# The recurrent layer of a two-layer decoder: head features stacked as high and low parts, scores in one rounded-f32 pass

## The chip, the core and the metric

The kernel runs on one core of a Trainium2 chip. TensorE (PE in the rows, PEld its weight loads) multiplies matrices, VectorE (DVE) and ScalarE (ACT) work elementwise, GpSimd (POOL) does so too and cannot touch the matmul results' memory (PSUM), SyncE (SP) issues DMAs. The metric is the time of one execution on the device in microseconds, the median of several.

## The reference

Two decoder layers over 4 batches of 256 tokens, width 256. Everything but the cross mixer of the second layer stays as it is. That mixer is a recurrent layer (an mLSTM) in its parallel form, with 16 heads of 16 features; the query is x, key and value are both the context:

```python
x3 = jnp.concatenate([q, k, v], axis=-1)
ig = (x3 @ Wi + bi).transpose(0, 2, 1)[..., None]
fg = (x3 @ Wf + bf).transpose(0, 2, 1)[..., None]
log_f = jax.nn.log_sigmoid(fg)             # cumulated over the tokens: fg_mat
log_D = log_fg + jnp.transpose(ig, (0, 1, 3, 2))      # causal, -inf above
max_log_D = jnp.max(log_D, axis=-1, keepdims=True)
D = jnp.exp(log_D - max_log_D)
qk = jnp.einsum('bhsd,bhtd->bhst', qh, kh) / jnp.sqrt(dh)
C = qk * D
normalizer = jnp.maximum(jnp.abs(C.sum(-1, keepdims=True)), jnp.exp(-max_log_D))
h = jnp.einsum('bhst,bhtd->bhsd', C / (normalizer + EPS), vh)
mu = h.mean(-1, keepdims=True)
hn = (h - mu) * jax.lax.rsqrt(((h - mu) ** 2).mean(-1, keepdims=True) + EPS) * ln_scale
```

## The kernel before

The program is a row of blocks; all engines meet at the end of each. Three blocks matter. In `layer1_lstm_load` SP issues two DMAs, and the block ends when they are issued. In `layer1_gates` PE forms both gates for all batches (L1241), ACT the log sigmoid, and VectorE the cumulated sums and maxima (L1276 to L1283), then the negated maximum in three bf16 parts (L1286 to L1293). SP copies these parts to rows of `nM_rows` with 12 DMAs (L1312), and the block ends when they have landed.

`layer1_lstm` is the recurrence: 4 batches of 16 heads, 64 heads in all, with keys on the partitions and queries along the row. The first and the last batch are written out, the two between are a loop. For each head:

- PE writes the exponent `l_z_ps` with two bf16 matmuls (L1386 the causal mask, L1387 the maximum), and ACT takes exp of it into `l_dec` in two instructions (L1471, L1472). Only 384 of 512 columns are needed, since the keys 128 to 255 are seen by the later queries alone.
- VectorE multiplies the transposed context by a column that is nonzero on the 16 rows of the head (`l_key`, L1502), and PE multiplies these 128 rows by xT in plain f32 (L1395 256 columns, L1397 128): the scores `l_qk_ps`.
- VectorE multiplies `l_dec` by `l_qk_ps` to `l_C` (L1554).

After four heads PE mixes the values with `l_C` (`mix`, L1414, 12 matmuls on 32 columns of the array), ACT keeps the result (L1453), PE turns it (L1423), ACT keeps that in `l_raw` (L1460). After a batch VectorE normalizes each head (13 instructions in `take`, `spread` and `scale`, L1508 to L1531), with one power on GpSimd (L1376, `l_rstd`) between them; they stand behind heads 4, 7 and 15 of the next batch. Each engine takes its instructions strictly in the order written. PE runs at most two heads ahead of VectorE, since the scores have two buffers; exponents and `l_dec` have four. Semaphores name what is waited for: `z_done`, `exped`, `qk_done`, `C_done`, `mixed`, `hT_kept`, `raw_kept`.

## Time and profile before

| | us |
|---|---|
| median of 3 runs (lowest, highest) | 1420.99 (1420.01, 1421.34) |
| span of the profiled execution | 1414.4 |
| what the median has beside the span | 6.6 |
| load block, first DMA issued | 914.3 |
| gates: first matmul, last DMA issued | 915.7, 944.0 |
| recurrence: first matmul, last result `h` | 945.7, 1052.5 |
| PE, VectorE, ACT, GpSimd busy in one batch of it (974 to 998) | 21.5, 19.9, 13.4, 5.5 of 24 |
| granted TensorE clock there | 1.00 of 2.4 GHz |

Only the three blocks differ between the kernels, so their stretch, 914 to 1053 us, is what is to be read. A time in a row is in us from the start of the span, durations follow it; in brackets stands how long the engine was idle before the instruction, and what ended that.

### The profile page before, as it was taken

To read this page: it belongs to the slowest core of one execution; us is meant where nothing else is said; L and a number is where in the kernel's file an instruction comes from. 1 tells how busy PE (TensorE), PEld (TensorE's weight loads), DVE (VectorE), ACT (ScalarE), POOL (GpSimd) and SP (SyncE) were. 2 spreads that over 40 slices of the span, in tenths; PEclk is the share of its full clock that TensorE was granted. 3 is DMA by queue.
4 is the path that set the end of the run, shared out by engine and by line. 5 is a ranking of instruction groups with operands and counts; after the bars stand their busy time and mean duration, and the time that the engine had idled before them with its cause. 6 is when DMAs were issued, how large, how long until landed. Compare 5 with 4: busy or idle time off the path is not lost. (4 is left out here: it accounts for less than half of the span.)

```text
span 1414.4 us, 20117 instructions
## 1 busy us (share of the span) xinstructions
PE 1156.9 (82%) x6280; PEld 883.5 (62%) x6280; DVE 723.0 (51%) x1850; ACT 480.2 (34%) x1324; POOL 411.8 (29%) x468
## 2 busy tenths in 40 slices
PE   5999999999660999086999999869946849999994
PEld 3777777778530887033777778737723537777773
DVE  5777787863440233220555561137864426566564
ACT  0333333341200232022555551125531234454442
POOL 3555555523535122640000000101141032342211
PEclk9999999999865899578999999979976879999997
DMA  9300000000012897214000000000001041112000
GB/s 334 146 23 22 22 22 22 11 1 1 1 37 89 267 299 252 83 43 144 10 14 12 12 1 1 19 5 2 0 1 36 1 134 45 45 52 83 0 1 30
DMA packets 72976, 82.16 MB, mean 58 GB/s; under 512 B 8417, under 2 KB 63527, under 8 KB 72912
## 3 DMA queue, kind: packets, MB, share of 16 engines
q1 hardware_dynamic: 59200, 50.94, 11.9%
q0 software_dynamic: 5632, 15.73, 3.2%
q10 hardware_dynamic: 8080, 14.69, 2.8%
q8 instruction: 34, 0.56, 0.2%
q14 instruction: 30, 0.25, 0.1%
HBM read 60.22 MB, written 22.02 MB: 58 GB/s over the span
## 5 line engine op out<-in xcount | busy, mean ns | idle before, releaser
L346 PE MATMUL a_proj_ps<-xT,a_w 128*128 128x512 f32 x256 | 121.8, 610 | 9.7 <-DMA a_w<-in_L_attn_Wv_dram 9.5
L248 ACT ACTIVATE a_probs<-a_score_ps,a_nmax 128x128 f32<-128x128 f32 x128 | 47.1, 368 | 207.3 <-DVE a_nmax L241 207.3
L221 PEld LDWEIGHTS a_turn_ps<-ident,a_probs 128*128 128x128 f32 x384 | 47.9, 142 | 65.7 <-DVE a_probs L259 32.8
L438 POOL TENSOR_TENSOR a_qk<-a_by_cos,a_by_sin 128x512 f32<-128x512 f32 x64 | 85.2, 1330 | 5.0
L104 POOL TENSOR_SCALAR ln_d_var<-ln_d_ssq 128x1 f32<-128x1 f32 x8 | 1.5, 192 | 283.6 <-ACT ln_d_sq L98 283.4
L221 PE MATMUL a_turn_ps<-ident,a_probs 128*128 128x128 f32 x384 | 65.0, 279 | 22.0 <-DVE a_probs L259 22.0
L346 PEld LDWEIGHTS a_proj_ps<-xT,a_w 128*128 128x128 f32 x256 | 47.3, 195 | 55.3 <-issue 49.8
L265 ACT ACTIVATE a_probsT<-a_turn_ps 128x384 f32<-128x384 f32 x128 | 62.5, 488 | 54.4 <-PE a_turn_ps L221 54.4
L240 DVE TENSOR_REDUCE a_nmax<-a_score_ps 128x1 f32<-128x128 f32 x128 | 36.6, 286 | 76.3 <-PE a_score_ps L214 75.7
L340 PEld LDWEIGHTS a_proj_ps<-a_w,xT 128*128 128x128 f32 x512 | 63.7, 196 | 15.5 <-issue 7.4
L434 POOL TENSOR_TENSOR a_by_sin<-a_swapped,sin_q 128x512 f32<-128x512 f32 x32 | 40.7, 1271 | 112.1 <-DVE a_swapped L394 112.1
L899 DVE TENSOR_TENSOR e_actT<-e_silu,e_up_ps 128x256 f32<-128x256 f32 x32 | 13.5, 421 | 113.0 <-ACT e_silu L883 113.0
L340 PE MATMUL a_proj_ps<-a_w,xT 128*128 128x128 f32 x512 | 64.2, 280 | 6.1 <-DVE a_swapped L394 6.1
L258 DVE TENSOR_SCALAR a_probs<-a_probs,a_rtotal 128x128 f32<-128x128 f32 x128 | 65.6, 512 | 4.5
L1092 PE MATMUL a_proj_ps<-xT,a_w 128*128 128x512 f32 x128 | 61.5, 605 | 3.2 <-DMA a_w<-in_L_attn_w_q_dram 3.2
L843 PE MATMUL e_up_ps<-e_rowsT,e_w 128*128 128x256 f32 x256 | 63.5, 393 | 0.0
L2111 DVE TENSOR_TENSOR m_xe<-m_xe_ps,xT 128x512 f32<-128x512 f32 x32 | 21.9, 691 | 79.4 <-PE m_xe_ps L1854 64.1
L833 PE MATMUL e_turn_ps<-ident,e_rows 128*128 128x128 f32 x128 | 21.2, 292 | 47.4 <-DMA e_rows<-slots 47.4
L259 DVE TENSOR_SCALAR a_probs<-a_probs,a_rtotal 128x256 f32<-128x256 f32 x128 | 59.6, 466 | 0.0
L250 ACT ACTIVATE a_probs<-a_score_ps,a_nmax 128x256 f32<-128x256 f32 x128 | 59.6, 466 | 0.0
L1177 PE MATMUL p_y_ps<-wo,attnT 128*128 128x256 f32 x256 | 55.5, 379 | 0.8 <-PEq L1071 0.8
L527 PE MATMUL t_y_ps<-wo,attnT 128*128 128x256 f32 x256 | 55.9, 379 | 0.0
(373 smaller groups left out, 3140.9 us busy)
## 6 DMA issues: line engine op xcount, KB each, us to landing
slots<-zeros ACTq DMA_DIRECT2D x4, 2048.0 KB, 16.6
e_rows<-slots SPq DMA_DIRECT2D x32, 256.0 KB, 4.2
e_w<-in_L_ffn_w_dram SPq DMA_DIRECT2D x32, 256.0 KB, 3.8
out_slots<-e_out POOLq DMA_DIRECT2D x32, 256.0 KB, 4.8
e_w<-in_L_ffn_w_dram SPq DMA_DIRECT2D x32, 128.0 KB, 3.8
m_up_w<-in_up_dram SPq DMA_DIRECT2D x8, 512.0 KB, 3.9
a_w<-in_L_attn_Wq_dram SPq DMA_DIRECT2D x16, 128.0 KB, 2.2
a_w<-in_L_attn_Wk_dram SPq DMA_DIRECT2D x16, 128.0 KB, 2.3
```

Source lines behind the costliest of these rows:

```text
L221: last = pe.transpose(self.turn_ps[:, r, j * P:(j + 1) * P], self.probs[:, r, j * P:(j + 1) * P], self.k.ident[:, :])
L250: act.activation(self.probs[:, r, P:P + S], self.score_ps[:, r, P:P + S], ACT.Exp, bias=self.nmax[:, r, 1:2], accum_out=self.total[:, r, 1 ...
L258: dve.tensor_scalar(self.probs[:, r, 0:P], self.probs[:, r, 0:P], self.rtotal[:, r, 0:1], None, ALU.mult)
L259: dve.tensor_scalar(self.probs[:, r, P:P + S], self.probs[:, r, P:P + S], self.rtotal[:, r, 1:2], None, ALU.mult).then_inc(self.normed, 1)
L265: act.activation(self.probsT[:, b % 2, :], self.turn_ps[:, b % 2, 0:CAUSAL], ACT.Copy).then_inc(self.turned_kept, 1)
L340: last = pe.matmul(proj_ps[:, c % 2, t * HD:(t + 1) * HD], k.xT[:, kc, half * HALF + t * P:half * HALF + (t + 1) * P], w[:, par, 2, kc, :] ...
L346: last = pe.matmul(proj_ps[:, c % 2, :], w[:, par, 0 if what == "q" else 1, kc, :], k.xT[:, kc, half * HALF:(half + 1) * HALF], start=kc = ...
L438: pool.tensor_tensor(qk[:, par, 0 if what == "q" else 1, half * HALF:(half + 1) * HALF], by_cos[:, r, :], by_sin[:, r, :], ALU.add).then_i ...
L527: last = pe.matmul(y_ps[:, t % 2, 0:D], k.ctxT[:, h, t * P:(t + 1) * P], k.wo[:, h, :], start=h == 0, stop=h == H - 1)
L843: last = pe.matmul(up_ps[:, r % 2, j * CAP:(j + 1) * CAP], w13[:, r, c, j * I0:(j + 1) * I0], rowsT[:, r % 2, c * CAP:(c + 1) * CAP], star ...
L1092: last = pe.matmul(proj_ps[:, half, :], w[:, par, c, :], k.xT[:, c, half * HALF:(half + 1) * HALF], start=c == 0, stop=c == DC - 1)
L1177: last = pe.matmul(y_ps[:, t % 2, 0:D], k.ctxT[:, h, t * P:(t + 1) * P], k.wo[:, h, :], start=h == 0, stop=h == H - 1)
```

## The change

- **Stacks.** The scores no longer use a masked key. `key_stack` holds the 16 key features of a head four times on 64 rows: twice their high part (rounded f32, F32R) and twice the rest (low part). `x_stack` holds the query features as high, low, high, low. One pass over 64 rows then sums all four products. Two heads lie on one tile of 128 rows, so the matmul of an odd head uses the lower half of the array (`tile_position`).
- **Building `x_stack`.** In the gates block ACT rounds a spreading matrix and x, VectorE takes the low part of x, PE spreads both with 32 F32R matmuls of 512 columns, ACT copies five results and VectorE three.
- **Building `key_stack`.** The context comes in stacked order from DRAM, 1 MB a batch, into two buffers (`raw`, in the place of the attention's output weights `wo`). ACT rounds a batch (`stack_high`, 128x8x256), then GpSimd subtracts on rows 32 to 63 and on rows 96 to 127 (`stack_low`, twice 32x8x256). Batch 0 is built in the gates block, batch 1 at the start of the recurrence, batches 2 and 3 when ACT has reached head 8 of the batch before.
- **Recurrence.** `l_key` and its instruction are gone. All 64 heads are written out. The scores have three buffers, the exponents three, `l_dec` six. The mask matmul writes 256 columns in place of 384. `mix` comes behind the scores of head n+2 when n % 4 is 1; ACT keeps its results behind exp of a head with n % 4 = 0.
- **Group norm.** The same 13 instructions are spread over heads 9 to 14 of the next batch, and the last two come behind head 6 of the batch after that; for the third batch they come after the last head.
- **Loads.** SP issues three more DMAs in the load block (the spreading matrix and two raw batches), and two in the recurrence.

```diff
+def stack_load(sp, k, I, b):
+
+    sp.dma_start(k.raw[:, b % 2], I["ctx_stack"][:, b * S:(b + 1) * S].rearrange("(c p) s -> p c s", p=P)
+                 ).then_inc(k.raw_in[b % 2], 16)
+
+
+def stack_high(act, k, b):
+
+    act.wait_ge(k.raw_in[b % 2], 16 * (b // 2 + 1))
+    act.activation(k.key_stack[:, :, b * S:(b + 1) * S], k.raw[:, b % 2], ACT.Copy).then_inc(k.stack_high, 1)
+
+
+def stack_low(pool, k, b):
+
+    pool.wait_ge(k.stack_high, b + 1)
+    for i, rows in enumerate((slice(P // 4, P // 2), slice(3 * P // 4, P))):
+        at_least(pool, k.stack_low, 2 * b + i)
+        pool.tensor_tensor(k.key_stack[rows, :, b * S:(b + 1) * S], k.raw[rows, b % 2],
+                           k.key_stack[rows, :, b * S:(b + 1) * S], ALU.subtract).then_inc(k.stack_low, 1)
...
+                pe.wait_ge(spread_ready, 1)
+                pe.wait_ge(x_low, DC)
+                for c in range(STACKS):
+                    at_least(pe, kept_a, min(c - 1, BY_ACT))
+                    at_least(pe, kept_v, c - 1 - BY_ACT)
+                    for half in range(2):
+                        tokens = slice(half * HALF, (half + 1) * HALF)
+                        for part, x in enumerate((x_p.h, x_p.l)):
+                            last = pe.matmul(st_ps[:, c % 2, half, :], k.spread[:, part, c % 4, :],
+                                             x[:, c // 4, tokens], start=part == 0, stop=part == 1)
+                    last.then_inc(stacked, 1)
...
+                act.wait_ge(k.spread_in, 16)
+                act.activation(k.spread[:, :, :, :], k.spread_w[:, :, :, :], ACT.Copy).then_inc(spread_ready, 1)
+                act.wait_ge(k.xT_ready, k.xT_count)
+                for c in range(DC):
+                    act.activation(x_p.h[:, c, :], k.xT[:, c, :], ACT.Copy).then_inc(x_high, 1)
...
+                stack_high(act, k, 0)
+                for c in range(BY_ACT):
+                    act.wait_ge(stacked, c + 1)
+                    act.activation(k.x_stack[:, c, :], st_ps[:, c % 2].rearrange("p a s -> p (a s)"), ACT.Copy
+                                   ).then_inc(kept_a, 1)
...
+                for c in range(DC):
+                    dve.wait_ge(x_high, c + 1)
+                    dve.tensor_tensor(x_p.l[:, c, :], k.xT[:, c, :], x_p.h[:, c, :], ALU.subtract).then_inc(x_low, 1)
...
+                for c in range(BY_ACT, STACKS):
+                    dve.wait_ge(stacked, c + 1)
+                    dve.tensor_copy(k.x_stack[:, c, :], st_ps[:, c % 2].rearrange("p a s -> p (a s)")
+                                    ).then_inc(kept_v, 1)
...
             def _(pool):
                 pool.memset(k.nM_rows[:, :, :], 0.0).then_inc(v_zero, 1)
+                pool.wait_ge(v_zero, 1)
+                stack_low(pool, k, 0)
...
-    RING = 4
+    RING = 3
+    DECS = 6
     GROUP = P // VW
     GROUPS_B = LH // GROUP
     NQ = QT * LH
+    STRIP = 4 * LW
...
+        STEPS = 11
+        AT_HEAD = {9: (0, 1, 2, 3), 10: (4,), 11: (5, 6), 12: (7,), 13: (8,), 14: (9,)}
...
+            @block.sync
+            def _(sp):
+                for b in range(2, B):
+                    sp.wait_ge(k.stack_low, 2 * (b - 1))
+                    stack_load(sp, k, I, b)
+
             @block.gpsimd
             def _(pool):
                 pool.memset(v_b[:, :, :, :], 0.0).then_inc(v_clear, 1)
                 pool.wait_ge(v_clear, 1)
                 pool.memset(v_b[:, :, :, LW:LW + 1], 1.0).then_inc(v_ones, 1)
+                pool.wait_ge(v_ones, 1)
+                stack_low(pool, k, 1)
                 for b in range(B):
+                    if b + 2 < B:
+                        at_least(pool, rstd_done, b)
+                        stack_low(pool, k, b + 2)
                     pool.wait_ge(var_done, b + 1)
+                    at_least(pool, k.stack_low, 2 * (b + 3) if b + 2 < B else 0)
...
+                def exponents(n):
+
+                    if n >= LH * B:
+                        return
+                    b, h = n // LH, n % LH
+                    at_least(pe, exped, n - RING + 1)
+                    z = z_ps[:, n % RING, :]
+                    pe.matmul(z.rearrange("p (a s) -> p a s", a=2)[:, :, 0:P], k.ident_bf[:, :],
+                              k.after_bf[:, :].rearrange("p (a s) -> p a s", a=2), start=True, stop=False,
+                              skip_group_check=True)
+                    pe.matmul(z[:, 0:CAUSAL], k.sel[:, h, :], k.nM_rows[:, b, :], start=False, stop=True,
+                              skip_group_check=True).then_inc(z_done, 1)
+
+                def products(n):
+
+                    if n >= LH * B:
+                        return
+                    at_least(pe, C_done, n - RING + 1)
+                    b, h = divmod(n, LH)
+                    if h == 0:
+                        pe.wait_ge(k.stack_low, 2 * (b + 1))
+                    c, strip = h // 2, h % 2 * STRIP
+                    rows = slice(strip, strip + STRIP)
+                    for keys_at, x_at, to in ((b * S, slice(b * S, (b + 1) * S), slice(0, S)),
+                                              (b * S + P, slice(b * S + P, (b + 1) * S), slice(S, CAUSAL))):
+                        last = pe.matmul(qk_ps[:, n % RING, to], k.key_stack[rows, c, keys_at:keys_at + P],
+                                         k.x_stack[rows, c, x_at], start=True, stop=True, tile_position=(strip, 0))
+                    last.then_inc(qk_done, 1)
...
+                for n in range(RING - 1):
+                    exponents(n)
+                products(0)
+                products(1)
+                for n in range(LH * B):
+                    exponents(n + RING - 1)
+                    products(n + 2)
+                    G = n // GROUP - 1
+                    if n % GROUP == 1:
+                        if G >= 1:
+                            turn(G - 1)
+                        if G >= 0:
+                            mix(G)
+                turn(B * GROUPS_B - 2)
+                mix(B * GROUPS_B - 1)
+                turn(B * GROUPS_B - 1)
...
+                stack_high(act, k, 1)
+                for n in range(LH * B):
+                    b, h = n // LH, n % LH
+                    if n % LH == 0:
+                        act.wait_ge(batch_ready, b + 1)
+                    if h == LH // 2 and 0 < b < B - 1:
+                        stack_high(act, k, b + 1)
+                    act.wait_ge(z_done, n + 1)
+                    at_least(act, C_done, n - DECS + 1)
+                    act.activation(dec[:, n % DECS, 0:S], z_ps[:, n % RING, 0:S], ACT.Exp,
+                                   bias=g_b[:, b % 2, 0, h:h + 1])
+                    act.activation(dec[:, n % DECS, S:CAUSAL], z_ps[:, n % RING, S:CAUSAL], ACT.Exp,
+                                   bias=g_b[:, b % 2, 1, h:h + 1]).then_inc(exped, 1)
+                    G = n // GROUP - 2
+                    if n % GROUP == 0 and G >= 0:
+                        if G >= 1:
+                            keep_raw(G - 1)
+                        keep_hT(G)
...
+                    at_least(dve, exped, LH * (b - 1))
+                    dve.tensor_copy(g_b[:, b % 2], k.g_tok[:, :, ROWS * b:ROWS * b + LH]).then_inc(batch_ready, 1)
...
+                for n in range(LH * B):
+                    b, i = divmod(n, LH)
+                    h = i
+                    dve.wait_ge(exped, n + 1)
+                    dve.wait_ge(qk_done, n + 1)
+                    if n % GROUP == 0:
+                        at_least(dve, mixed, n // GROUP - 1)
+                    dve.tensor_tensor(C[:, h % (2 * GROUP), :], dec[:, n % DECS, :], qk_ps[:, n % RING, 0:CAUSAL],
+                                      ALU.mult).then_inc(C_done, 1)
+                    if b > 0:
+                        if i == 2:
+                            dve.wait_ge(mixed, GROUPS_B * b)
+                            values(b)
+                        for j in AT_HEAD.get(i, ()):
+                            group_norm(b - 1, j)
+                    if b > 1 and i == 6:
+                        for j in (10, 11):
+                            group_norm(b - 2, j)
+                    if i == 8 and b + 1 < B:
                         fetch(b + 1)
+                for j in (10, 11):
+                    group_norm(B - 2, j)
+                for j in range(12):
+                    group_norm(B - 1, j)
...
+            sp.dma_start(k.spread_w[:, :, :, :], I["spread"]).then_inc(k.spread_in, 16)
+            stack_load(sp, k, I, 0)
+            stack_load(sp, k, I, 1)
```

On TensorE, the heads around a mix in the first batch of before (`l_z_ps` exponents, `l_qk_ps` scores, `l_hT_ps` mix, `l_turn_ps` turn):

```order
L1386 MATMUL l_z_ps<-after_bf,ident_bf 128x384
L1387 MATMUL l_z_ps<-nM_rows,sel 128x384
L1414 MATMUL l_hT_ps<-l_C,l_v_b 32x128 x12
L1395 MATMUL l_qk_ps<-xT,l_key 128x256
L1397 MATMUL l_qk_ps<-xT,l_key 128x128
L1386 MATMUL l_z_ps<-after_bf,ident_bf 128x384
L1387 MATMUL l_z_ps<-nM_rows,sel 128x384
L1395 MATMUL l_qk_ps<-xT,l_key 128x256
L1397 MATMUL l_qk_ps<-xT,l_key 128x128
L1423 MATMUL l_turn_ps<-ident,l_hT 128x128 x2
```

and now:

```order
L1453 MATMUL l_z_ps<-after_bf,ident_bf 128x2x128
L1456 MATMUL l_z_ps<-nM_rows,sel 128x384
L1471 MATMUL l_qk_ps<-x_stack,key_stack 128x256
L1471 MATMUL l_qk_ps<-x_stack,key_stack 128x128
L1493 MATMUL l_turn_ps<-ident,l_hT 128x128 x2
L1485 MATMUL l_hT_ps<-l_C,l_v_b 32x128 x12
```

The mix has moved behind the scores, and the turn of the group before stands in front of it.

On GpSimd, everything in the gates block and the recurrence of before:

```order
L1304 MEMSET nM_rows 128x1536
L1371 MEMSET l_v_b 128x1024
L1373 MEMSET l_v_b 128x32
L1376 TENSOR_TENSOR l_rstd<-l_var,minus_half 128x32 x4
```

and now, where `key_stack<-wo,key_stack` is the subtraction of the low part (two a batch):

```order
L1360 MEMSET nM_rows 128x1536
L1225 TENSOR_TENSOR key_stack<-wo,key_stack 32x8x256 x2
L1428 MEMSET l_v_b 128x1024
L1430 MEMSET l_v_b 128x32
L1225 TENSOR_TENSOR key_stack<-wo,key_stack 32x8x256 x4
L1439 TENSOR_TENSOR l_rstd<-l_var,minus_half 128x32
L1225 TENSOR_TENSOR key_stack<-wo,key_stack 32x8x256 x2
L1439 TENSOR_TENSOR l_rstd<-l_var,minus_half 128x32 x3
```

The power of a batch now stands behind the subtractions for the batch after the next.

On VectorE, behind head 7 of the second batch, now:

```order
L1623 TENSOR_TENSOR l_C<-l_dec,l_qk_ps 128x384
L1563 COPY l_g_b<-g_tok 128x32
L1623 TENSOR_TENSOR l_C<-l_dec,l_qk_ps 128x384
L1576 SCALAR_TENSOR_TENSOR l_rnorm<-l_raw 128x32
L1579 TENSOR_TENSOR l_norm<-l_rnorm,least 128x32
L1581 TENSOR_SCALAR l_normed<-l_norm 128x32
L1583 RECIPROCAL l_rnorm<-l_normed 128x32
L1623 TENSOR_TENSOR l_C<-l_dec,l_qk_ps 128x384
L1585 TENSOR_TENSOR l_hv<-l_raw,l_rnorm 128x512
L1589 TENSOR_REDUCE l_hsum<-l_hv 128x32
L1623 TENSOR_TENSOR l_C<-l_dec,l_qk_ps 128x384
```

The copy of the gates for the next batch stands behind head 8, the group norm starts behind head 9, and no `l_key` stands between.

## Rows read from the trace of the kernel before

**Rows 1.** Windows: one batch; then a pause of TensorE, and ten microseconds later.

```profile
974.00:998.00 24.00, 21.48 (x207) 17.15 (x206) 19.91 (x51) 13.41 (x43) 5.47 (x1) 1.00 0.01 2
1090.00:1095.00 5.00, 1.10 (x3) 0.19 (x1) 4.76 (x8) 0.60 (x1) 0.00 (x0) 1.00 0.01 2
1100.00:1105.00 5.00, 4.31 (x22) 4.27 (x21) 0.00 (x0) 2.48 (x3) 0.00 (x0) 0.50 0.01 3
```

**Rows 2.** Timeline (start, duration, engine, line) around one mix of the recurrence.

```profile
988.38 0.33 PE L1386 MATMUL l_z_ps<-after_bf,ident_bf 128*128 128x384 bf16 x1
988.54 0.33 PE L1387 MATMUL l_z_ps<-nM_rows,sel 128*128 x1
...
988.79 0.86 PE L1414 MATMUL l_hT_ps<-l_C,l_v_b 128*32 128x128 f32 x24
...
989.59 0.70 PE L1395 MATMUL l_qk_ps<-xT,l_key 128*128 x2
...
990.00 0.47 ACT L1471 ACTIVATE l_dec<-l_z_ps,l_g_b 128x256 f32<-128x256 f32 x1
...
990.76 0.55 DVE L1554 TENSOR_TENSOR l_C<-l_dec,l_qk_ps 128x384 f32<-128x384 f32 x1 [1.30 <-ACT l_dec L1472]
...
991.24 0.35 DVE L1502 TENSOR_SCALAR l_key<-cT,head_of 128x256 f32 x1
```

**Rows 3.** Timeline of TensorE: two rounded-f32 matmuls of 256 columns.

```profile
1195.17 0.28 PE L1852 MATMUL m_down_ps<-m_down_l,m_act_h 128*128 128x256 f32 x1
1195.30 0.28 PE L1853 MATMUL m_down_ps<-m_down_h,m_act_h 128*128 128x256 f32 x1
```

**Rows 4.** Timeline: start of the recurrence, heads 0 and 16, the last two heads.

```profile
945.66 0.48 PE L1386 MATMUL l_z_ps<-after_bf,ident_bf 128*128 128x384 bf16 x1 [7.41 <-PEq L1232]
...
950.15 0.55 DVE L1554 TENSOR_TENSOR l_C<-l_dec,l_qk_ps 128x384 f32<-128x384 f32 x1 [1.02 <-PE l_qk_ps L1397]
...
971.43 0.56 DVE L1554 TENSOR_TENSOR l_C<-l_dec,l_qk_ps 128x384 f32<-128x384 f32 x1 [1.18 <-PE l_qk_ps L1397]
...
1036.93 1.18 DVE L1554 TENSOR_TENSOR l_C<-l_dec,l_qk_ps 128x384 f32<-128x384 f32 x2 [1.56 <-ACT l_dec L1472]
```

**Rows 5.** Timeline of the last group norm: first, power, last.

```profile
1040.49 0.21 DVE L1508 SCALAR_TENSOR_TENSOR l_rnorm<-l_raw 128x32 f32<-128x32 f32 x1 [1.06 <-ACT l_raw L1460]
...
1045.66 5.42 POOL L1376 TENSOR_TENSOR l_rstd<-l_var,minus_half 128x32 f32<-128x32 f32 x1 [10.33 <-DVE l_var L1526]
...
1051.83 0.69 DVE L1531 TENSOR_TENSOR h<-l_hs,head_scale 128x512 f32<-128x512 f32 x1
```

**Rows 6.** Instructions by tile (ns min/median/max): rounding on ACT, subtraction on GpSimd.

```profile
L2062 ACT ACTIVATE m_up_h<-m_up_w x8: 1039/1046/1046, 1143.0 to 1353.2; 128x1024 fp32r<-128x1024 f32 x8
L1970 POOL TENSOR_TENSOR m_up_l<-m_up_w,m_up_h x8: 2379/2409/2409, 1144.1 to 1354.3; 128x1024 fp32r<-128x1024 f32 x8
```

**Rows 7.** Timeline: VectorE while GpSimd works; then two of its lines by tile.

```profile
72.40 1.27 POOL L434 TENSOR_TENSOR a_by_sin<-a_swapped,sin_k 128x512 f32<-128x512 f32 x1
72.45 1.37 DVE L259 TENSOR_SCALAR a_probs<-a_probs,a_rtotal 128x256 f32<-128x256 f32 x1
...
L259 DVE TENSOR_SCALAR a_probs<-a_probs,a_rtotal x128: 340/348/1376, 35.3 to 849.8; 128x256 f32<-128x256 f32 x128
...
L2145 DVE TENSOR_TENSOR m_act<-m_silu,m_up x16: 676/677/1424, 1165.0 to 1388.7; 48x512 f32<-48x512 f32 x16
```

**Rows 8.** Timeline of the gates block, from the logarithm to the DMAs.

```profile
927.85 0.42 ACT L1260 ACTIVATE g_ln<-g_e 128x256 f32<-128x256 f32 x1
...
932.88 0.69 DVE L1283 TENSOR_TENSOR_SCAN g_M<-ones,g_g 128x256 f32<-128x256 f32 x1
...
933.60 0.29 DVE L1286 TENSOR_SCALAR g_nM<-g_M 128x256 f32<-128x256 f32 x1
...
936.42 7.58 SPq L1312 DMA_DIRECT2D nM_rows<-g_parts  x12
```

**Rows 9.** Timeline: the second DMA issue of the load block.

```profile
914.68 0.42 SPq L2243 DMA_DIRECT2D after_bf<-in_after_bf_dram  x1
```

234 lines of the change are left out of this document (83 added, 151 removed).

## The prediction

> **What bounds the kernel now.** I read the page first (its table stands above), then windows over the recurrence, then timelines in order of time. In a batch of 24 us TensorE is busy 21.5 and VectorE 19.9 at full clock [rows 1], so neither alone is the bound: they hand over to each other. Around a mix the reader sees how. The mix starts 0.25 us behind the exponents, holds TensorE 0.8 us (988.79 to 989.59), and VectorE sits idle 1.30 us until exp arrives [rows 2]. Batch 0 runs 21.3 us without a group norm (heads 0 to 16), all 64 heads take 88.0 us (950.15 to 1038.11), and the first head starts 4.5 us into the block [rows 4]. Behind the last head come 2.4 us until the last group norm starts, then 12.0 us to `h` [rows 5]. In the gates block the end is set by VectorE's chain: the maximum at 932.88, its negation from 933.60, 2.8 us to the last part, then 12 DMAs in 7.6 us, landed at 945.6 [rows 4, 8].
>
> **The change part by part.** The terms are differences to the profiled execution; the 6.6 us that the median has beside the span are taken as they are.
>
> *Loads, +1.4.* Three more issues stand before the end of the load block, at 0.42 us and a short gap each [rows 9]: 3 x 0.47.
>
> *Recurrence without disturbance, -26.6.* A rounded-f32 pass of 256 columns starts 0.13 us after the one before [rows 3]; I take 0.13 + 0.06 for the scores of a head (by column count for the narrow one; if it ran as four passes it would be 0.2, which adds 0.15 a group of four heads). The exponents take 0.16 for 384 columns [rows 2], so 0.11 + 0.16. VectorE needs for a head between 0.48 (next start behind an `l_C`) [rows 2] and 0.59 (half of 1.18) [rows 4], I take 0.5. Then a group of four heads runs in a loop that I close over the mix: end of `l_C` of head n-1, scores 0.2, turn 0.25 (two f32 transposes of 128 columns, an estimate from [rows 3]), mix with its start gap 0.25 + 0.8 [rows 2], exponents of head n+3 0.27 and 0.2 to their end, exp 0.76 (990.00 to 990.76) [rows 2], `l_C` 0.55: 3.3 us. The copies that ACT keeps of the results lie beside it. Batch 0 is four such groups and slower by 0.3 while the clock is low: 13.5. In later batches the group norm fills the gaps: its first ten steps take 5.2 us (1040.49 to 1045.66) [rows 5], the last two 1.4, the two copies 0.6. Heads 8 to 11 then cost VectorE 4 x 0.5 + 3.6 = 5.6, heads 12 to 15 2.0 + 1.7 = 3.7, heads 0 to 3 stay at 3.3, heads 4 to 7 take 3.3 (3.4 with the two late steps): 15.9, 16.0, 16.0. Sum 61.4 against 88.0.
>
> *Start of the recurrence, -1.6.* ACT first rounds batch 1: 1.046 us for 1024 elements [rows 6], so 2.0 for 2048. Exp is at 2.8, head 0 at 2.9 instead of 4.5 [rows 4].
>
> *Tail, +4.0.* The third batch's variance is now ready behind head 14 of the last batch. The power takes 5.4 us [rows 5], so its last two steps start 5.0 us behind the last `l_C` and end at 6.4, where the last group norm started at 2.4 before. All that follows is unchanged.
>
> *GpSimd against VectorE.* One subtraction of 128x1024 takes GpSimd 2.41 us [rows 6]; the new ones have 2048 elements on 32 partitions, I take 4.7 each (a little under twice), 9.4 a batch. What they do to VectorE decides. At 72.45 a `tensor_scalar` of VectorE that takes 0.35 alone takes 1.37, just until a subtraction-like instruction of GpSimd (72.40, 1.27 long) is over, and this line's maximum is 1.376 [rows 7]. A `tensor_tensor` with both inputs in SBUF shows the same (0.68 alone, 1.42 at most) [rows 7]. `l_C` reads PSUM, reductions and reciprocals have one input, and they should go on; nearly every other instruction of the group norm and of the gates chain is of the two kinds that wait. The Trainium skill says it outright (SBUF — State Buffer, section Who interferes with whom): VectorE instructions with two SBUF inputs, or in a two-port mode, exclude a GpSimd instruction that reads SBUF for its whole length, whichever comes first. The trace agrees at 1.27 us; that it holds at four times that length no row shows.
>
> - Gates, +6.7. ACT is through with the logarithm at 929.7 (1.4 late), rounds batch 0 until 931.6, GpSimd subtracts to 936.3. The maximum (two SBUF inputs) would start at 934.3, so it runs from 936.3 to 937.0; GpSimd's second subtraction has been queued since 936.4 and gets in first, as in the pair at 72.40. The negation starts at 941.7, the last part is ready 2.8 later at 944.5, where it would have been at 937.8 [rows 8]. Bounds: 0 if nothing excludes, 2.1 if the chain keeps its turn. The 32 matmuls, the eight copies of x and batch 0's subtractions end before the DMAs land.
> - Batch 0, +0.6: the copy of the gates behind head 8 meets the rest of batch 1's subtractions.
> - Batches 1 and 2, +7.8 and +8.1. ACT rounds the next batch when it reaches head 8, GpSimd starts at about `l_C` of head 8. Of its 9.4 us only heads 8 and 9 (some 1.6 us) run beside; the gate copy and the first group norm step wait for the rest, and all of the group norm comes afterwards.
> - Low clock after these pauses, +3.5. TensorE idles some 4 us twice. After a pause of about that size it is granted 0.50 at 86% busy [rows 1]: 1.2 of 2.4 GHz. At that level a group with a mix takes it 5.8 us (scores and exponents 3.6, turn and mix 2.2) against 3.3 to 5.6 that VectorE needs. I take 1.75 a pause; bounds 0 and 4.
>
> Sum: 1.4 - 26.6 - 1.6 + 4.0 + 6.7 + 16.5 + 3.5 = +3.9, so 1425.
>
> Another rule speaks against the change: the Trainium skill (TensorE: Matmul & The Clock Gate, section A second HAM failure mode: psum-queue depth-cycling) tells of a kernel in which brief idling between groups of matmuls made the clock swing. Here TensorE would be idle a quarter of the time even without the exclusions; the trace has no such stretch in the recurrence (clock 1.00) [rows 1]. It is the last rival.
>
> **The rivals.**
> *The exclusion costs half* (faster). GpSimd gets in only between VectorE's instructions or is shorter on 32 partitions, so the chain in the gates keeps its turn (2.1) and batches 1 and 2 lose 4 to 5 each, without a fall of the clock: 1.4 - 26.6 - 1.6 + 4.0 + 2.1 + 10 = -10.7, 1410. For it: the late instruction of VectorE gets its turn at once when GpSimd's ends. Against it: at 72.45 VectorE was 0.05 us late and waited the full length [rows 7], and the second subtraction is queued while VectorE still runs.
> *No exclusion* (clearly faster): the two streams pass each other, only the readiness of the low parts costs 2 us, since the subtractions end about when head 14 asks for the next batch: -26.6 - 1.6 + 1.4 + 4.0 + 2 = -20.8, 1400. Against it stand both lines of [rows 7].
> *The clock stays low* through the undisturbed groups too: 2.5 us (5.8 against 3.3) for each of ten groups without group norm, less the 3.8 that the sum has for it: +21 on the forecast, 1446; half of it 1435. For it: idle time of TensorE in every group; against it: the full clock at 21.5 of 24 us [rows 1], and that TensorE at 1.2 GHz would have no idle time left in these groups.
> Beside these, `values` of batch 0 may lose its turn to batch 1's first subtraction (VectorE leads by less than 0.1 us): +4, within the range. The change does what it says if the scores' matmuls are single passes; even as four passes it is only 1 to 2 us.
>
> **How the numbers follow.** Forecast 0.62 (own range 1416 to 1433), half exclusion 0.18 (1404 to 1416), none 0.10 (1395 to 1404), low clock 0.10 (1433 to 1448). The range 1407 to 1437 leaves out the third, a part of the second and half of the last. A measurement can tell 0.2%, 2.8 us, from no change: faster than 1418.2 are the second and third and a tenth of the first, 0.33; within, 0.17; slower, 0.50.
>
> **What would show it.** Right: subtractions of GpSimd near 4.7 us; the first group norm instruction behind head 9 with a duration of several us, ending with a subtraction; the negation in the gates block late by 6 to 7; in batch 3, where GpSimd subtracts nothing, 16 us; a granted clock below 1.00 in the second half of batches 1 and 2; the last group norm 6 to 7 us behind the last `l_C`. Wrong: group norm instructions of normal length beside subtractions (then 1400), GpSimd instructions that are themselves stretched, batches over 18 us without a subtraction.

## The result, and the profile after

The changed kernel takes 1439.5 us (median of 4 runs, 1434.4 to 1450.8) against 1420.5 (1416.1 to 1421.3) for the kernel before: a ratio of 1.016, 95% interval 1.012 to 1.021. Slower was right, but 19 us and not 4: the time lies 2.5 us outside the range of 1407 to 1437. It also varies from run to run by 16 us, where the kernel before varies by 5 in its four runs (by 10 and 12 in the 19 and 22 runs beside the first eight experiments).

The profiled execution of the changed kernel is the fastest of its four. The two profiled executions differ by 18.2 us in their spans (1432.6 and 1414.4), and `h` is complete 18.2 us later, so all of it arises up to the end of the recurrence:

| term | predicted | between the profiles |
|---|---|---|
| stages ahead of the changed blocks | 0 | +1.5 |
| loads | +1.4 | +1.6 |
| gates | +6.7 | +6.0 |
| start of the recurrence, to its first product | -1.6 | -1.8 |
| first to last product | -6.6 (88.0 to 81.4) | +6.6 (88.0 to 94.6) |
| tail, to `h` | +4.0 | +4.3 |

Every term that was forecast, but for the products, came out within 0.7 us. The 1.5 us ahead of the changed blocks are a difference that I can't assign.

The gates block, in the timeline of VectorE and GpSimd (start, duration, engine, line), answers to [rows 8]:

```profile
936.02 2.45 DVE L1335 TENSOR_TENSOR_SCAN g_M<-ones,g_g 128x256 f32<-128x256 f32 x1
938.51 4.51 DVE L1338 TENSOR_SCALAR g_nM<-g_M 128x256 f32<-128x256 f32 x1
...
933.36 9.50 POOL L1225 TENSOR_TENSOR key_stack<-wo,key_stack 32x2048 fp32r<-32x2048 f32 x2 [13.41 <-ACT key_stack L1217]
```

The scan takes 2.45 us instead of 0.69 and ends with GpSimd's first subtraction; the second gets in ahead of the negation, which takes 4.51 instead of 0.29 and ends with it at 942.9. In batch 1 (VectorE's timeline; the subtractions run from 983.86 to 992.95) the reader sees the same twice, then an instruction of normal length once GpSimd is through:

```profile
984.91 3.51 DVE L1563 COPY l_g_b<-g_tok 128x32 f32<-128x32 f32 x1
988.33 0.54 DVE L1623 TENSOR_TENSOR l_C<-l_dec,l_qk_ps 128x384 f32<-128x384 f32 x1
988.80 4.22 DVE L1576 SCALAR_TENSOR_TENSOR l_rnorm<-l_raw 128x32 f32<-128x32 f32 x1
993.05 0.19 DVE L1579 TENSOR_TENSOR l_norm<-l_rnorm,least 128x32 f32<-128x32 f32 x1
```

TensorE over the same time, in the windows view (columns: window, its length, then busy time and count of instructions for TensorE's matmuls, its weight loads, VectorE, ACT and GpSimd, granted clock, DMA share, GB/s), answers to [rows 1]:

```profile
954.00:966.00 12.00, 11.25 (x58) 5.85 (x58) 4.86 (x10) 7.43 (x17) 9.85 (x4) 0.50 0.26 87
967.00:982.00 15.00, 15.00 (x151) 8.86 (x154) 8.73 (x17) 11.76 (x39) 0.00 (x0) 1.00 0.22 72
988.00:990.00 2.00, 0.82 (x4) 0.41 (x4) 2.00 (x3) 0.00 (x0) 1.92 (x2) 1.00 0.00 0
992.00:998.00 6.00, 3.25 (x11) 1.77 (x11) 5.83 (x13) 2.44 (x8) 0.95 (x1) 0.50 0.00 1
998.00:1022.00 24.00, 24.00 (x155) 12.82 (x154) 14.16 (x20) 12.31 (x32) 12.99 (x3) 0.50 0.00 1
1022.00:1037.00 15.00, 13.08 (x75) 7.19 (x78) 10.02 (x20) 6.77 (x20) 6.91 (x2) 0.50 0.00 1
1038.00:1050.00 12.00, 11.46 (x102) 6.56 (x100) 10.13 (x23) 9.43 (x30) 0.00 (x0) 1.00 0.00 1
```

The clock is at 0.50 (1.2 GHz) in the first 12 us of the recurrence, falls again in the pause of batch 1 (in windows of 2 us it is 1.00 from 988, 0.55 from 990 and 0.50 from 992), and then stays there for 47 us, 24 of them with TensorE busy in all of the 24. The products of batches 0 to 3 take 18.0, 26.1, 30.5 and 19.9 us. A group with its mix takes 7.1 us there. And at full clock a group takes 4.2, not 3.3. TensorE's timeline shows why:

```profile
974.20 0.28 PE L1453 MATMUL l_z_ps<-after_bf,ident_bf 128*128 128x256 bf16 x1
974.32 0.33 PE L1456 MATMUL l_z_ps<-nM_rows,sel 128*128 128x384 bf16 x1
974.57 0.44 PE L1471 MATMUL l_qk_ps<-x_stack,key_stack 64*128 64x256 f32 x2
974.95 0.28 PE L1453 MATMUL l_z_ps<-after_bf,ident_bf 128*128 128x256 bf16 x1
```

From start to start a head takes 0.75 us: 0.12, then 0.25 (0.16 by its 384 columns) until the scores start, then 0.38 (0.16 by columns) until the next exponents. I had 0.47. Four times 0.75, 0.37 for the turn and 0.80 for the mix are the 4.2: TensorE has become the bound.

### The profile page after: what moved, and what is told of

The parts are those of the page before. It is cut to its first block and busy times, and to the rows that moved or that the text cites. A ratio compares the mean times of both kernels' runs of the same rounds, so it can differ in the third digit from the quotient of the medians.

```text
span 1432.6 us, 19649 instructions
## 1 busy us (share of the span) xinstructions
PE 1166.2 (81%) x6184; PEld 870.3 (61%) x6184; DVE 730.1 (51%) x1791; ACT 494.9 (35%) x1336; POOL 448.0 (31%) x476
## 5 line engine op out<-in xcount | busy, mean ns | idle before, releaser
L340 PEld LDWEIGHTS a_proj_ps<-a_w,xT 128*128 128x128 f32 x512 | 63.7, 196 | 15.5 <-issue 7.4
## 6 DMA issues: line engine op xcount, KB each, us to landing
slots<-zeros ACTq DMA_DIRECT2D x4, 2048.0 KB, 17.1
```

Of the source, the lines that this page charges most:

```text
L340: last = pe.matmul(proj_ps[:, c % 2, t * HD:(t + 1) * HD], k.xT[:, kc, half * HALF + t * P:half * HALF + (t + 1) * P], w[:, par, 2, kc, :] ...
```

## The experiments

In the texts on record a "theory" is what I held at that moment. Times are medians, with the lowest and highest run behind them; the kernel before was measured beside them each time (medians 1416.7 to 1417.6), and ratios are to these. What I read off each trace first is the time from the first to the last product (88.0 before, 94.6 after) and the stretches at 0.50.

**1. Small subtractions** (`x1_small_low`). The low parts are left out but for 8 columns:

```diff
-        pool.tensor_tensor(k.key_stack[rows, :, b * S:(b + 1) * S], k.raw[rows, b % 2],
-                           k.key_stack[rows, :, b * S:(b + 1) * S], ALU.subtract)
+        pool.tensor_tensor(k.key_stack[rows, 0, b * S:b * S + 8], k.raw[rows, b % 2, 0, 0:8],
+                           k.key_stack[rows, 0, b * S:b * S + 8], ALU.subtract)
```

> The changed kernel, but GpSimd's subtractions of the low part run over 8 columns of one chunk instead of 2048 elements (most low parts are left out; everything else is as it was). Theory: GpSimd's long instructions hold up VectorE (6.0 us in the gates block, 7.3 and 6.5 in batches 1 and 2), the two pauses of TensorE that follow take its clock to 0.50, and with the pauses gone it stays at 1.00 from about 966 on: a group of four heads takes 4.2 us instead of 7.1, batches 1 to 3 about 17 us each instead of 25, 30.5 and 19.9. Sum -6 -24 = 1409, clock 1.00 from the tenth microsecond of the recurrence to its end. Rival 1 (the clock falls by the new instruction mix itself, 64-row scores and no key masks, whatever pauses): the gates lose their 6 us, but the clock goes down again somewhere in batch 1 and batches take 25 to 28 us: 1433 or more. Rival 2 (the chip lowers the clock while GpSimd runs its long instructions, and they make no one wait): as the theory in time, but then the warmed kernel of this call would not help.

Measured: 1415.2 (1408.5 to 1423.2), ratio to before 0.999 (0.997 to 1.002); 87.6 us for the products. So by the medians the subtractions cost 24 us in all, give or take 8 by the two intervals; the profiled executions differ by 15.4, 7.0 of it in the products. But the clock did not do what the theory said:

```profile
948.00:1002.00 54.00, 53.85 (x311) 28.65 (x311) 22.67 (x48) 29.60 (x77) 5.19 (x7) 0.50 0.13 40
1003.00:1037.00 34.00, 32.25 (x323) 18.70 (x326) 26.50 (x58) 26.77 (x80) 7.21 (x4) 1.00 0.01 1
```

Without any pause it is at 0.50 from the start for 54 us, at 53.85 us of busy TensorE, and then at 1.00. No pause is needed for it to stay low. This speaks for the cause that rival 1 names, though not for its 1433. The second window also gives batches at full clock without exclusion: 18.5 and 17.1 us between the products of heads 32, 48 and the last.

**2. Idle matmuls in the pauses** (`x3_warm`), in batches 1 and 2 ahead of the scores:

```diff
+    def filler(n, count):
+        if count:
+            pe.wait_ge(exped, n + 1)
+        for _ in range(count):
+            pe.matmul(z_ps[:, n % RING, 0:S], k.ident_bf[:, :], k.after_bf[:, :], start=True, stop=True)
+    FILL = {9: 16, 10: 40}
...
+    if n // LH in (1, 2):
+        filler(n, FILL.get(n % LH, 0))
```

> The changed kernel with idle matmuls for TensorE in its two pauses: behind head 9 sixteen and behind head 10 forty bf16 matmuls of 256 columns, in batches 1 and 2 alone, into a bank that the next exponents overwrite. The exclusion stays as it is (7.3 and 6.5 us). Theory (the pause of TensorE, and nothing else, takes the clock down, and in the mix of this recurrence it doesn't come back before 1037): the clock stays at 1.00, batch 1 as long as now or 1 us longer, batch 2 about 24.5 instead of 30.5, batch 3 17 instead of 19.9, so 1430. Rival (GpSimd's load, or the mix of work, sets the clock): the clock falls in spite of the matmuls, which then take up to 24 us themselves at 0.43 us less each: 1440 to 1450.

Measured: 1439.1 (1432.8 to 1445.1), as the changed kernel. The trace shows two opposite things, which cancel in the time. This execution was at 0.50 for 40 us from 952, where the changed kernel's was for 12 at its start, and its batches 0 and 1 took 23.9 and 30.2 us instead of 18.0 and 26.1. But with the pauses filled the clock stayed at 1.00 through both of them, and batches 2 and 3 took 25.2 and 17.1 us instead of 30.5 and 19.9, as the theory has them. So a pause does take the clock down in this mix. The idle matmuls did not bring it back: it rose at 993, over 2 us ahead of the first of them (995.5). In between it fell once more, for 3 us from 1007, with TensorE busy for 2.58 of the 3 us before.

```profile
952.00:992.00 40.00, 38.52 (x216) 20.62 (x220) 14.16 (x28) 22.07 (x57) 10.37 (x4) 0.50 0.16 54
993.00:1006.00 13.00, 12.89 (x112) 9.13 (x110) 11.65 (x14) 5.96 (x19) 8.80 (x2) 0.99 0.00 1
```

**3. Scores over all rows** (`x4_full_rows`). Each score adds up two heads:

```diff
-    last = pe.matmul(qk_ps[:, n % RING, to], k.key_stack[rows, c, keys_at:keys_at + P],
-                     k.x_stack[rows, c, x_at], start=True, stop=True, tile_position=(strip, 0))
+    last = pe.matmul(qk_ps[:, n % RING, to], k.key_stack[:, c, keys_at:keys_at + P],
+                     k.x_stack[:, c, x_at], start=True, stop=True)
```

> The changed kernel, but each score matmul takes all 128 rows of the stacks instead of the 64 of one head (it adds up the scores of two heads; the same columns, the same number of instructions, no place on the array given). In the trace of the changed kernel a head takes TensorE 0.75 us at full clock: 0.12 and 0.25 for the exponents, 0.38 for the scores, where my sum had 0.47. Theory (the place on the array costs: the weights for 64 rows can't be loaded while a 128-row matmul still runs, 0.1 us in front of the first and 0.1 in front of the second): a head takes 0.55 to 0.60, a group 3.5 instead of 4.2, and with more rows in use the clock comes back sooner after a pause; 1439 - 16 groups x 0.6 = 1429 or less. Rival (a rounded-f32 pass has this cost anyway, by its weight load of 0.19 us or by a second pass): 0.75 a head stays, and so does 1439.

Measured: 1419.1 (1416.4 to 1423.0), the theory and more, 20 us less than the changed kernel with the same subtractions and pauses; 79.9 us for the products. In TensorE's timeline a head now takes 0.48, and the scores start at once:

```profile
971.90 0.28 PE L1453 MATMUL l_z_ps<-after_bf,ident_bf 128*128 128x256 bf16 x1
972.02 0.33 PE L1456 MATMUL l_z_ps<-nM_rows,sel 128*128 128x384 bf16 x1
972.05 0.48 PE L1471 MATMUL l_qk_ps<-x_stack,key_stack 128*128 128x256 f32 x2
972.38 0.28 PE L1453 MATMUL l_z_ps<-after_bf,ident_bf 128*128 128x256 bf16 x1
```

(A weight load ahead of its turn is counted with its matmuls, so their start is too early by a little; the distance from exponents to exponents is what counts.) Behind each pause the clock is at 0.50 too, but it is back 6 to 8 us after TensorE starts again (956.3 to 962.2, 990.2 to 996.3, 1015.7 to 1023.8). In windows:

```profile
956.00:962.00 6.00, 5.74 (x25) 4.79 (x26) 3.01 (x7) 5.38 (x12) 4.42 (x3) 0.50 0.52 175
962.00:980.00 18.00, 16.46 (x213) 12.78 (x210) 13.02 (x22) 15.87 (x46) 6.00 (x2) 0.99 0.19 60
...
988.00:996.00 8.00, 4.72 (x36) 3.05 (x36) 7.83 (x17) 2.63 (x8) 1.35 (x1) 0.50 0.00 1
996.00:1006.00 10.00, 8.92 (x106) 6.44 (x98) 6.53 (x13) 8.99 (x25) 6.21 (x2) 0.98 0.01 2
```

**4. The kernel before, with the subtractions' time added** (`x8_before_excl`), behind head 9 of batches 1 and 2:

```diff
+    pool.wait_ge(exped, LH * (b + 1) + 9)
+    for i in range(2):
+        pool.tensor_tensor(idle_b[0:32, :], idle_a[0:32, :], idle_b[0:32, :], ALU.subtract)
```

> The kernel before, with two more GpSimd subtractions over 2048 elements on 32 rows from when ACT has passed head 9, in batches 1 and 2, on tiles of their own that nobody needs: the same 9.1 us of GpSimd as in the changed kernel. Theory: VectorE's instructions of two SBUF inputs wait for them (about 4 us each time one meets one: +4 to +8 a batch), TensorE pauses, and its clock falls to 0.50; at 90% busy in this older mix of full-row matmuls it comes back after about 8 us, as at the start of the recurrence (945 to 953), so +3 for each: 1420.5 + 12 + 6 = 1438. Rival 1 (any pause of this size costs the clock until near the end, whatever the mix): +25 to +35. Rival 2 (nothing of the exclusion carries over because the group norm stands elsewhere there): 1420 to 1425.

Measured: 1435.8 (1434.4 to 1438.6), ratio 1.0145 (1.012 to 1.017): the theory. The products take 104.2 us. The exclusion is at work here too, in the timelines of VectorE and GpSimd:

```profile
995.49 2.75 DVE L1513 TENSOR_SCALAR l_key<-cT,head_of 128x256 f32 x1
998.16 0.54 DVE L1565 TENSOR_TENSOR l_C<-l_dec,l_qk_ps 128x384 f32<-128x384 f32 x1
998.62 4.59 DVE L1541 TENSOR_TENSOR l_hs<-l_hc,l_rstd 128x512 f32<-128x512 f32 x1
...
993.43 9.23 POOL L1387 TENSOR_TENSOR l_idle_b<-l_idle_a,l_idle_b 32x2048 f32<-32x2048 f32 x2
```

With its full-row scores the clock is back soon: in windows of 2 us, TensorE starts again in that from 1006, at 0.50, and has 0.55 in that from 1010 and 1.00 behind it; the second time it is 5 us. Behind its pause in batch 1 the changed kernel stayed at 0.50 for 47 us.

**5. Gates and tail** (`x26_gates_tail`).

```diff
                 pool.wait_ge(v_zero, 1)
+                pool.wait_ge(nm_done, 1)
                 stack_low(pool, k, 0)
...
-                for j in (10, 11):
-                    group_norm(B - 2, j)
-                for j in range(12):
-                    group_norm(B - 1, j)
+                for j in range(10):
+                    group_norm(B - 1, j)
+                for b in (B - 2, B - 1):
+                    for j in (10, 11):
+                        group_norm(b, j)
```

> The changed kernel with two edits far apart, read apart in the trace. In the gates block GpSimd's first two subtractions wait until VectorE has made the negated maximum and the last `nm`; in the tail the last two steps of the third batch stand between the last batch's variance and its scaling, in the 5.4 us in which VectorE waits for the power. Theory: the maximum's scan takes 0.7 instead of 2.45 and the negation 0.3 instead of 4.51, the last part is ready 6.0 earlier and the recurrence starts 6 earlier; the last group norm starts 2.4 behind the last product instead of 6.6, so 4.2 less in the tail. Rival for the gates: the subtractions only move behind, and hold up the copies and the turned gates until the block ends as late as before: 0 to 2 gained. Rival for the tail: the power of the third batch itself is late for the last batch's, 0 gained. Sum by the theory -10; where the clock of TensorE comes back differs from run to run by up to 40 us (in the trace of the changed kernel it was at 0.50 for 59 us, in the other runs more), so 1422 to 1436.

Measured: 1437.2 (1428.7 to 1443.9). By the time alone this is inconclusive. In the trace scan and negation are short again:

```profile
934.27 0.69 DVE L1335 TENSOR_TENSOR_SCAN g_M<-ones,g_g 128x256 f32<-128x256 f32 x1
934.99 0.29 DVE L1338 TENSOR_SCALAR g_nM<-g_M 128x256 f32<-128x256 f32 x1
```

The last part is ready 6.0 us earlier, as the theory has it: from the start of the scan to the first DMA 3.6 us (934.27 to 937.82) instead of 9.5 (936.02 to 945.55). Of these the recurrence gets 4.9: from the scan to its first matmul 13.8 us instead of 18.7. GpSimd's two subtractions, moved behind, end at 947.8, just ahead of that matmul (948.1), so the rival holds for 1.1 us. The first product comes at 950.8 instead of 957.5, but 1.8 us of this lie ahead of the scan.

But the profiled execution was at 0.50 from 952 to the end of the recurrence: 110.2 us for the products, the worst case of the changed mix. Since mix and turn are slow then, the last group norm starts 5.4 us behind the last product; the tail is to be read in experiment 8.

**6. No exclusion at all** (`x7_best`). VectorE makes the low part over 128 rows at once, and the work stands where engines are free:

```diff
-    act.activation(k.key_stack[...], k.raw[:, b % 2], ACT.Copy)
+    act.activation(k.key_stack[...], k.raw[:, b % 2], ACT.Identity, scale=k.flip[:, 0:1])   # -1 high, +1 low rows
...
+    dve.scalar_tensor_tensor(k.key_stack[:, at, ...], k.raw[:, b % 2, at], k.is_low[:, 0:1],
+                             k.key_stack[:, at, ...], ALU.mult, ALU.subtract)                  # four pieces
+    HIGH_AT = {8: 2, 18: 3}
+    LOW_AT = {1: 1, 2: 1, 3: 1, 4: 1, 9: 2, 10: 2, 11: 2, 12: 2, 20: 3, 21: 3, 22: 3, 23: 3}
```

> A version of the changed kernel without the exclusion: the low part is made by VectorE with one instruction over all 128 rows in four pieces of 0.7 us a batch (ACT rounds with the sign turned on the high rows, and VectorE takes raw x 0 or 1 less that), batch 0 in the shadow of the DMAs in the gates block, the others between heads of batches 0 and 1; batch 1 is rounded in the gates block; the tail as in the kernel beside it. Theory: as the kernel with small subtractions (1415.2) less the tail's 4.2 and the 2 us of the rounding: 1409, and as there the clock of TensorE is at 0.50 from the start of the recurrence for 10 to 55 us, since a mix of 64-row scores doesn't bring it back. Rival: VectorE's pieces, 8 us in all, are not hidden and eat the gain: 1415 or more.

Measured: 1410.8 (1398.4 to 1413.0), ratio 0.994 (0.992 to 0.996), faster than before; 0.50 for the 38 us from 952, then 1.00; products 81.2 us. As the theory.

**7. The same, warmed** (`x12_best_warm`): `for _ in range(60)` an idle matmul at the end of TensorE's part of the gates block.

> The same version with sixty idle bf16 matmuls of 256 columns for TensorE at the end of the gates block, while the DMAs of the negated maximum are on their way (6.4 us at full clock, 13 at half). Theory (the mix of the recurrence can keep the clock but hardly wins it back): the recurrence starts at 1.00 and stays there, since no pause comes, a group takes 4.2 us all through: 67 to 69 us from the first to the last product against 94.6 in the changed kernel, so 1401. Rival (the mix itself can't keep the clock): it falls in the first 20 us of the recurrence all the same, and the time is that of the kernel beside it, 1409, or 5 more if the matmuls run at half clock and are not done when the block ends.

Measured: 1412.8 (eleven runs from 1405.1 to 1418.1, one of 1430.6), no better. The theory falls, the rival holds. The recurrence does start at 1.00, and the clock falls all the same, twice, without a pause: TensorE was busy for 4.57 of the 6 us before the first fall (at 958) and for 3.30 of the 4 us before the second.

```profile
948.00:956.00 8.00, 6.96 (x58) 5.15 (x55) 0.76 (x3) 2.41 (x8) 1.10 (x2) 1.00 0.22 70
...
958.00:972.00 14.00, 14.00 (x85) 7.62 (x86) 9.33 (x18) 8.84 (x21) 0.00 (x0) 0.52 0.23 75
972.00:988.00 16.00, 15.81 (x164) 9.04 (x163) 11.47 (x26) 13.10 (x37) 0.00 (x0) 1.00 0.01 3
988.00:992.00 4.00, 3.30 (x28) 1.90 (x31) 3.93 (x9) 3.25 (x10) 0.00 (x0) 1.00 0.01 2
992.00:1008.00 16.00, 16.00 (x111) 8.48 (x100) 7.58 (x16) 6.91 (x21) 5.43 (x1) 0.50 0.00 1
```

**8. No exclusion, and full rows** (`x9_best_full`). x is kept twice, the other head's 64 rows at zero, so that a 128-row matmul yields one head:

```diff
+    pool.memset(k.x_stack[rows, at].bitcast(F32), 0.0)
-    k.key_stack[rows, c, keys_at:keys_at + P], k.x_stack[rows, c, x_at], ..., tile_position=(strip, 0)
+    k.key_stack[:, c, keys_at:keys_at + P], k.x_stack[:, h % 2, c, x_at], ...
```

> The version without the exclusion, and scores over all 128 rows: x is kept twice, with the other head's 64 rows at zero (GpSimd clears them, ACT and VectorE make 16 copies of 1.0 us instead of 8). Theory: a head takes TensorE 0.47 instead of 0.75 (0.46 to 0.47 in the kernel with full rows), a group some 3.3 to 3.5 instead of 4.2, limited by VectorE and by the loop over the mix, and the clock is back within 6 to 8 us of the start, as in the kernel with full rows: 62 to 65 us from the first to the last product, 1395 to 1398. Rival 1: the doubled copies of x don't fit beside the DMAs of the gates block and push the start by up to 8 us: 1403 to 1406. Rival 2: with TensorE faster VectorE (0.5 a head, 5.2 for a group norm, 2.8 for a batch's low part) is the bound and nothing more than 3 us is won over the version with 64 rows at full clock: 1399.

Measured: 1399.7 (1399.0 to 1400.3), ratio 0.987 (0.985 to 0.990): 18 us faster than the kernel before and 40 than the changed one, and without its scatter. The products take 63.8 us, and TensorE starts at 954, and the clock is up from 958.5:

```profile
952.00:957.00 5.00, 3.05 (x14) 2.51 (x14) 2.19 (x6) 1.83 (x6) 1.11 (x2) 0.50 0.39 124
957.00:1020.00 63.00, 52.55 (x633) 37.50 (x632) 54.84 (x119) 52.28 (x154) 10.87 (x2) 0.99 0.08 25
```

TensorE is idle a sixth of the 63 us and keeps its clock. The last group norm starts 2.4 us behind the last product (1020.5 to 1022.9), as before, and the third batch's last steps lie in the wait for the power: the tail's 4.2 us are gone. The products are faster by more than the 3 us of rival 2: 63.8 against the 69.4 that 64-row scores need at full clock (worked out below). Rival 1 holds for 6 us, which are still to be had here: the copies of x end at 952.6, and from the maximum's scan to the first product it takes 21.6 us (935.1 to 956.7) instead of the 15.5 of experiment 6 (938.0 to 953.5).

**9. The same, warmed** (`x13_full_warm`), with the sixty matmuls.

> The version with full rows (1399.7) and the sixty idle matmuls at the end of the gates block. Its recurrence ran at 0.50 for its first 4 to 5 us only, and TensorE has idle time in every window of it. Theory: those few microseconds become 1.00 and 1 to 2 us are won, 1398, if the matmuls are over when the DMAs have landed. Rival: they are not over (they stand behind the turned gates, and the copies of x run until 953 here), and push the start: 1402 to 1405.

Measured: 1406.7 (1402.7 to 1407.5), 7 us slower: the rival. The clock is at 1.00 from 946 on, but the products take the same 63.8 us, and the first of them comes at 960.1, 3.4 us late. In this mix the few cold microseconds cost nothing that shows. The profiled execution is 3.2 us longer in span than that of experiment 8, which is this delay; what adds the rest in the median is open.

**10. One idle matmul a head** (`x16_best_fill`), added to the version of experiment 6:

```diff
     exponents(n + RING - 1)
+    if n < LH * B - 2:
+        pe.wait_ge(exped, n + 1)
+        pe.matmul(z_ps[:, n % RING, 0:S], k.ident_bf[:, :], k.after_bf[:, :], start=True, stop=True)
     products(n + 2)
```

> The version without the exclusion and with 64-row scores (1410.8, clock 0.50 from 954 to 990) with one idle 128-row bf16 matmul of 256 columns more for each head: 0.11 us of TensorE at full clock, 64 x 0.11 = 7 us in all, if TensorE is the bound. TensorE was at 3.9 to 4.0 of 4 us busy in the stretches in which its clock fell (at 958 and 992 in the version with warmed start), so idle time is not the cause there. Theory A (what keeps the clock is work on all rows of the array; 64-row matmuls count for less): the clock is back within 10 us and stays at 1.00, a group takes 4.6, the recurrence some 75 us against the 80 of the version without them, so 1405. Theory B (the mix with its weight loads and turns sets the clock, whatever is added; only denser time helps, as 40 such matmuls in a row did): the clock stays low as long as before, and the matmuls cost 0.2 each at 0.50: 1418 to 1425.

Measured: 1405.3 (1402.5 to 1408.2), ratio 0.991 (0.989 to 0.993), the number of theory A: more work for TensorE, and 5.6 us less time by the medians.

```profile
948.00:966.00 18.00, 18.00 (x100) 9.99 (x100) 11.27 (x21) 9.40 (x23) 0.40 (x2) 0.50 0.33 108
966.00:1024.00 58.00, 58.00 (x566) 35.30 (x564) 42.92 (x92) 42.85 (x128) 10.86 (x2) 0.99 0.01 2
```

Its mechanism the trace bears out in part: the clock is back after 20 us, sooner than the 37 of experiment 6 but not within 10, and the products take 78.5 us against 81.2, where the theory had 75 against 80. (The text on record has TensorE busy for 3.9 to 4.0 of 4 us around the two falls of experiment 7; from 956 to 960 and from 990 to 994 it is 3.6 and 3.5.)

**11. One place on the array** (`x17_one_strip`): `strip` is 0 for all heads, so odd heads get the scores of the head before them.

> The same version with 64-row scores, but all heads take rows 0 to 63 at the place (0, 0) (odd heads get the scores of the head before them). Theory A (64 rows cost the 0.28 us a head by their weight load, wherever they lie: the load can't run beside a 128-row matmul): 0.75 a head as before, 1410. Theory B (the change between the two places, 0 and 64, costs it): the second matmul of a head and the exponents behind it no longer wait, 0.47 to 0.6 a head: 1400 to 1405.

Measured: 1412.1 (1406.5 to 1414.3), theory A. In TensorE's timeline the head is as long as with two places:

```profile
1013.82 0.28 PE L1453 MATMUL l_z_ps<-after_bf,ident_bf 128*128 128x256 bf16 x1
1013.93 0.33 PE L1456 MATMUL l_z_ps<-nM_rows,sel 128*128 128x384 bf16 x1
1014.19 0.44 PE L1471 MATMUL l_qk_ps<-x_stack,key_stack 64*128 64x256 f32 x2
1014.57 0.28 PE L1453 MATMUL l_z_ps<-after_bf,ident_bf 128*128 128x256 bf16 x1
```

It is not the change from row 0 to row 64 that costs 0.28 us a head, but the change from 128-row to 64-row matmuls and back. The start of the recurrence shows this a second way. There the scores of heads 0 and 1 stand one behind the other, at full clock, first in experiment 6 (rows 0 and 64), then here (rows 0 for both):

```profile
951.43 0.45 PE L1471 MATMUL l_qk_ps<-x_stack,key_stack 64*128 64x256 f32 x4
951.81 0.28 PE L1453 MATMUL l_z_ps<-after_bf,ident_bf 128*128 128x256 bf16 x1
...
948.29 0.67 PE L1471 MATMUL l_qk_ps<-x_stack,key_stack 64*128 64x256 f32 x4
948.89 0.28 PE L1453 MATMUL l_z_ps<-after_bf,ident_bf 128*128 128x256 bf16 x1
```

The scores of one head hold TensorE for 0.38 us, those of two heads at the same rows for 0.60, and those of two heads at rows 0 and 64 for 0.38, as if there were one. So a second head of 64 rows without a change of mode adds 0.22 at the same place and nothing at the other. The Trainium skill has this rule (TensorEngine Tiling (Array Packing), section Key Properties): a change of the tiling mode drains TensorE, a change of the tile alone does not. Both halves of it agree with the traces here (0.75 us a head with both changes, with two places as with one, and 0.48 with 128 rows throughout); the rule stood there before the prediction, and I had not drawn on it.

**12. One idle matmul of 64 rows a head** (`x18_half_fill`): as experiment 10, with rows 0 to 63.

> As the version with one idle matmul a head (1405.3), but the idle matmul takes 64 rows at (0, 0) instead of 128: the same 256 columns, and TensorE as busy. Theory A (rows in use count for the clock): this matmul adds half as much, the clock is at 0.50 about as long as in the version without idle matmuls (35 us there, 16 us in the one with 128 rows) or falls again later, and the time is above 1410, up to 1420. Theory B (columns or busy time count, whatever the rows): the clock comes back as soon as with 128 rows, 1405, or 1407 with a weight load that isn't hidden.

Measured: 1404.1 (1397.9 to 1413.5). By its median theory B, by its trace theory A: the profiled execution is one of its slow ones (span 1409.0) and is at 0.50 from 948 to 988. The seven runs here scatter by 15.6 us (by 5.7 with 128 rows), so the medians don't decide. This one stays open.

## Why the prediction was wrong

**Loads, gates, start, tail: right**, each within 0.7 us of its term. GpSimd's subtraction took 4.55 to 4.75 us (4.7 taken), it held up VectorE for its whole length, and the second one got in ahead, as put.

**Batches 1 and 2, +7.8 and +8.1: right in mechanism, a little less in size.** The held-up instructions cost 3.3 + 4.0 and, in batch 2, 2.5 + 4.0 us beyond their normal lengths: 13.8 instead of 16.5 with batch 0's 0.6 (there the copy took its normal 0.17). This is a sum of instruction lengths, though, and not all of it is lost: TensorE was idle for 6.7 of the 10 us from 986, but in batch 2 only for 1.9 of the 6 us from 1022, since at 0.50 its own work, four groups of 7.1, fills 28.4 of the 30.5 us. That the exclusion costs VectorE and not only GpSimd is shown by experiments 1, 4 and 5. No exclusion and half of it, the two faster rivals, are out.

**Recurrence without disturbance, -26.6: the step that failed.** I took 0.2 us for the scores of a head and 0.27 for the exponents. The single pass was right (0.48 a head with 128 rows, experiment 3), but both changes between 128-row and 64-row matmuls come on top: 0.75 (experiments 3 and 11). With 16.7 us for batch 0 (four groups of 4.2) and 17.1, 18.5 and 17.1 for the others (experiment 1, batch 1 taken as batch 3) the undisturbed recurrence at full clock is 69.4 us, not 61.4. With full rows the sum does come out: 63.8, VectorE's low parts included.

**Low clock, +3.5: the second miss, which came with the same 64-row scores.** What is left of the 94.6 us, 94.6 - 69.4 - 13.8, is 11.4, a remainder and not a measurement; with TensorE's idle time (8.6) in the place of the 13.8 it would be 16.6. Either is beyond the bounds of 0 and 4 a pause. The three together are the miss: 8.0 for the undisturbed recurrence and 7.9 for the clock, less 2.7 for the held-up instructions, make 13.2 of the products' 94.6 - 81.4. "TensorE at 1.2 GHz would have no idle time left" was right (24.00 of 24.00 us busy), but that this brings the clock back was not. The rival that had the clock stay low, at 0.10, named the effect, with the wrong cause: it put it down to idle time, and the clock stayed low in stretches without any (experiment 1). That it fell in the pauses was right (experiment 2); how long it stayed down was not. In the traces the recurrence was at 0.50 for 12 + 47 us (changed kernel) and for 54, 40, 38, 36 and 110 us (experiments 1, 2, 6, 11, 5), 14 and 17 in experiment 7, with 64-row scores alone, and for 4 to 8 us behind each start of TensorE with full rows (experiments 3, 4, 8). This goes with the scatter of the changed kernel's time: its four runs of 1434.4, 1437.2, 1441.7 and 1450.8 us have a mean granted clock of 0.886, 0.882, 0.878 and 0.876. Why 64-row scores keep it down, and for how long, stays open.

**What is not shown.** That the number of array rows in use is what the clock goes by: the full-row versions differ from the others in density too, since their heads are shorter, and have no changes of mode around the scores, and experiments 10 and 12 don't part these in their medians. Pairs of heads, scored one behind the other at rows 0 and 64, ran at the start of the recurrence only (experiment 11): there exponents and scores of two heads took 1.01 us, 0.5 a head. What they would do to the whole kernel and its clock was not tried.

## What to carry to other kernels

A matmul on part of the rows between full ones isn't cheaper: price it from start to start in a mix of both, and where memory allows, pad one operand with zeros and stay at 128 rows (experiment 8), or try to set such matmuls side by side, at rows 0 and 64 one behind the other. A long GpSimd instruction with two full SBUF operands must be placed as if VectorE ran it, and what it holds up costs time only as far as VectorE's lateness reaches the engine that bounds the stretch. And where TensorE becomes the bound at a clock that can be 0.50, the time of every matmul is to be taken at both levels.
